# Attention loads in half as many DMAs, score tiles ahead of the maxima, first loads in another order

## The reference

```python
x = _layernorm(x + _L0_attn_ref(x, ...))       # causal self-attention
x = _layernorm(x + _L0_xattn_ref(x, ctx_768, ...))   # attention to the context
x = _layernorm(x + _L0_ffn_ref(x, ...))        # soft mixture: 8 experts x 128 slots
x = _layernorm(x + _L1_attn_ref(x, ...))       # causal
x = _layernorm(x + _L1_xattn_ref(x, ctx_768, ...))   # context
x = _layernorm(x + _L1_ffn_ref(x, ...))        # x + causal attention, then + top-2 of 8 experts
```

## Time and profile before

| | |
|---|---|
| median of 3 runs | 3067.17 us (3059.79 to 3073.33) |
| the profiled execution | 3064.33 us, its span 3062.5 us |
| PE busy | 2568.9 us, 84% |
| DVE busy | 1499.4 us, 49% |
| ACT busy | 1346.1 us, 44% |
| POOL busy | 457.8 us, 15% |
| mean granted clock of PE, share of full speed | 0.916 |
| DMA, mean over the span | 85 GB/s |

### The profile page before, as it was taken

How to read it: one execution, slowest core, us unless ns; L and a number is a source line. 1 busy time by engine, 2 the same in 40 slices (tenths; PEclk the granted TensorE clock), 3 DMA queues, 4 the chain that set the end, 5 groups by cost and what they waited for, 6 DMA issues and landing times. The chain is left out here.

```text
span 3062.5 us, 48054 instructions
## 1 busy us (share of the span) xinstructions
PE 2568.9 (84%) x15793; PEld 1469.9 (48%) x15794; DVE 1499.4 (49%) x4196; ACT 1346.1 (44%) x2886; POOL 457.8 (15%) x719
## 2 busy tenths in 40 slices
PE   4999999999828979998588999898987986489992
PEld 2555544444314446676355544343434554356671
DVE  0555677888425420013444487777744564222223
ACT  2555456666634432211244456665754553022220
POOL 3222212101110000000112212212122000500004
PEclk7899999999969999999699999999998997599996
DMA  8344664454000012203644465354422332711102
GB/s 205 97 126 126 131 118 82 68 73 73 1 17 1 1 59 88 87 17 137 158 109 123 111 128 80 56 101 62 92 59 60 103 83 95 249 31 34 34 30 89
DMA packets 184550, 259.98 MB, mean 85 GB/s; under 512 B 32952, under 2 KB 106944, under 8 KB 184256
## 3 DMA queue, kind: packets, MB, share of 16 engines
q1 hardware_dynamic: 181264, 248.85, 34.5%
q0 software_dynamic: 3072, 8.39, 0.9%
HBM read 180.71 MB, written 81.53 MB: 86 GB/s over the span
## 5 line engine op out<-in xcount | busy, mean ns | idle before, releaser
L1345 ACT ACTIVATE second_p<-psum 128x512 f32<-128x512 f32 (+3 forms) x1024 | 461.7, 520 | 287.9 <-PE psum L1211 284.3
L1345 ACT ACTIVATE first_p<-psum 128x512 f32<-128x512 f32 (+3 forms) x768 | 365.7, 547 | 179.1 <-PE psum L1211 176.5
L1419 DVE TENSOR_REDUCE first_max_parts<-psum 128x1 f32<-128x512 f32 x512 | 323.0, 684 | 74.7 <-PE psum L1188 72.1
L1419 DVE TENSOR_REDUCE second_max_parts<-psum 128x1 f32<-128x512 f32 x512 | 321.9, 683 | 72.9 <-PE psum L1188 70.2
L1415 DVE CUSTOM_DVE_ANT_0 second_masked<-psum,mask_qk 128x384 f32<-128x384 f32 (+3 forms) x512 | 230.0, 489 | 230.7 <-PE psum L1188 189.1
L1201 PE MATMUL psum<-second_q,second_k 64*128 64x512 f32 (+3 forms) x1024 | 227.7, 440 | 42.1 <-DVE second_max_parts L1419 26.2
L1188 PE MATMUL psum<-second_k,second_q 64*128 64x512 f32 (+3 forms) x1024 | 203.7, 395 | 67.5 <-DMA second_k<-a_k_parts 51.5
L1223 PE MATMUL psum<-second_p,second_v_aug 128*32 128x512 f32 (+3 forms) x2048 | 240.1, 542 | 8.3 <-ACT second_p L1345 8.1
L1188 PE MATMUL psum<-first_k,first_q 64*128 64x512 f32 (+3 forms) x768 | 158.0, 411 | 61.7 <-ACT first_held L1382 26.0
L1201 PEld LDWEIGHTS psum<-second_q,second_k 64*128 64x128 f32 x1024 | 98.8, 188 | 230.1 <-issue 83.6
L1415 DVE CUSTOM_DVE_ANT_0 first_masked<-psum,mask_qk 128x128 f32<-128x128 f32 (+3 forms) x256 | 114.8, 488 | 179.7 <-PE psum L1188 152.5
(11 more groups left out here) (317 smaller groups left out, 3819.2 us busy)
## 6 DMA issues: line engine op xcount, KB each, us to landing
first_k<-c_k_parts SPq DMA_DIRECT2D x128, 128.0 KB, 5.7
second_q<-a_q_parts SPq DMA_DIRECT2D x256, 64.0 KB, 2.8
second_k<-a_k_parts SPq DMA_DIRECT2D x256, 64.0 KB, 2.9
second_k<-c_k_parts SPq DMA_DIRECT2D x128, 128.0 KB, 5.6
first_q<-a_q_parts SPq DMA_DIRECT2D x128, 64.0 KB, 2.9
first_k<-a_k_parts SPq DMA_DIRECT2D x128, 64.0 KB, 2.9
c_k_parts<-first_held SPq DMA_DIRECT2D x16, 512.0 KB, 3.2
first_q<-c_q_parts SPq DMA_DIRECT2D x128, 64.0 KB, 5.3
```

Of the source, the lines that this page charges most:

```text
L1345: evacuated(act.activation(probs[tile % 2][:, 2 * h + p, q0:SEQ], bank[:, q0:SEQ], ACT.Exp, scale=scale), event)
L1419: evacuated(v.reduce_max(max_parts[n % 2][:, h, p, qt, k0 // BANK:k0 // BANK + 1], bank[:, 0:width], axis=AX_X), event)
```

## The change

Four edits.

1. The plan: a step writes both score tiles, then all its units, then the values of tile t-1 (or the last values and the drain of group n-1), and then the chain steps and pieces.
2. `load(n)` issues 8 DMAs in place of 16, each for 32 partitions. The weights' columns (and biases) of queries and keys are put in another order on the host (`by_heads`), so that the two heads of a row pair follow each other within a partition; the buffer holds the two contiguously (`keys_of`). A group's bytes stay the same, and so do the matmuls.
3. The weights: in the first stage the first layer's are issued at the start as before, the others at a new event "weights", which stands after load 2; in the second all stand after loads 0 to 3. In the first stage load 0 and vload 0 now stand after the first slot's projections, the other first loads after the second slot's. The first contexts are loaded later.
4. `stage_experts`: two semaphores in place of one, so that the first matmul waits for the up matrix and its bias alone.

```diff
         for t in range(steps):
             plan.append(("scores", n, (t, 0)))
-            share(units, 2 * t + 1, 2 * steps)
-            if t:
-                plan.append(("values", n, t - 1))
-            elif n:
-                plan.extend([("values", n - 1, layer_of(n - 1).key_tiles - 1), ("drain", n - 1, 0)])
             if t == 1:
                 if n:
                     plan.append(("turn", n - 1, 0))
...
             plan.append(("scores", n, (t, 1)))
             share(units, 2 * t + 2, 2 * steps)
+            if t:
+                plan.append(("values", n, t - 1))
+            elif n:
+                plan.extend([("values", n - 1, layer_of(n - 1).key_tiles - 1), ("drain", n - 1, 0)])
...
+        def keys_of(n):
+            keys = layer_of(n).keys
+            return ks[n % NB][:, :, :].rearrange("p i t -> p (i t)")[:, 0:2 * keys].rearrange("p (i t) -> p i t", i=2)
...
-                for dst, src, columns in own_loads:
-                    sp.dma_start(dst, src, allow_slow_non_contiguous=columns).then_inc(own_in, 16)
-                for dst, src, columns in later_loads:
-                    sp.dma_start(dst, src, allow_slow_non_contiguous=columns).then_inc(later_in, 16)
+                def fetch_weights(loads, done):
+                    for dst, src, columns in loads:
+                        sp.dma_start(dst, src, allow_slow_non_contiguous=columns).then_inc(done, 16)
+
+                if not layers[0].projected:
+                    fetch_weights(own_loads, own_in)
...
-                        for blk, (qp, kp) in enumerate(((0, 0), (0, 1), (1, 0), (1, 1))):
-                            at = slice(64 * h + HD * blk, 64 * h + HD * (blk + 1))
-                            sp.dma_start(qs[n % NB][at, :, :].bitcast(F32),
-                                         q_dram[qp, row:row + 2 * HD, :].rearrange("(i d) t -> d i t", d=HD)
-                                         ).then_inc(stack_in[n % NB], 16)
-                            sp.dma_start(ks[n % NB][at, :, 0:layer.keys].bitcast(F32),
-                                         k_dram[kp, row:row + 2 * HD, :].rearrange("(i d) t -> d i t", d=HD)
-                                         ).then_inc(stack_in[n % NB], 16)
+                        for half in range(2):
+                            at = slice(64 * h + 2 * HD * half, 64 * h + 2 * HD * (half + 1))
+                            sp.dma_start(qs[n % NB][at, :, :].bitcast(F32).rearrange("p i t -> p (i t)"),
+                                         q_dram[half, row:row + 2 * HD, :].rearrange("(d i) t -> d (i t)", i=2)
+                                         .unsqueeze(0).to_broadcast([2, HD, 2 * SEQ])
+                                         ).then_inc(stack_in[n % NB], 16)
+                            sp.dma_start(ks[n % NB][at, :, :].rearrange("p i t -> p (i t)")[:, 0:2 * layer.keys].bitcast(F32),
+                                         k_dram[:, row:row + 2 * HD, :].rearrange("a (d i) t -> a d (i t)", i=2)
+                                         ).then_inc(stack_in[n % NB], 16)
...
+                    elif event[0] == "weights":
+                        if layers[0].projected:
+                            fetch_weights(own_loads, own_in)
+                        fetch_weights(later_loads, later_in)
...
-                        pe.wait_ge(stack_in[r], 256 * (n // NB + 1))
+                        pe.wait_ge(stack_in[r], 128 * (n // NB + 1))
...
-        pieces = {-3: front_pieces(a0, 0, "x") + FIRST_LOADS, -2: front_pieces(a0, 1, "x")}
+        pieces = {-3: front_pieces(a0, 0, "x") + FIRST_LOADS[:2],
+                  -2: front_pieces(a0, 1, "x") + FIRST_LOADS[2:5] + [("weights", 0, 0), ("load", 3, 0)]}
...
-        contexts = {-3: [("context", BATCH, 0), ("context", BATCH + 1, 0)]}
+        contexts = {-1: [("context", BATCH, 0), ("context", BATCH + 1, 0)]}
...
-        pieces = {-3: FIRST_LOADS}
-        contexts = {-3: [("context", BATCH, 0), ("context", BATCH + 1, 0)]}
+        pieces = {-3: FIRST_LOADS + [("weights", 0, 0)]}
+        contexts = {-2: [("context", BATCH, 0), ("context", BATCH + 1, 0)]}
```

More of the change, by code:

```diff
@@ L1188, in unit @@
                         ins = pe.matmul(bank_of(event, h)[:, 0:width], qs[r][own, p, qt * P:(qt + 1) * P],
-                                        ks[r][own, p, k0:k0 + width], start=True, stop=True)
+                                        keys_of(n)[own, p, k0:k0 + width], start=True, stop=True)
                         filled(ins, event)
@@ L1200, in scores @@
                         own = slice(64 * h, 64 * h + 64)
-                        pe.matmul(bank_of(event, h)[:, q0:SEQ], ks[r][own, p, t * P:(t + 1) * P],
+                        pe.matmul(bank_of(event, h)[:, q0:SEQ], keys_of(n)[own, p, t * P:(t + 1) * P],
                                   qs[r][own, p, q0:SEQ], start=True, stop=False)
@@ L1563, in stage_experts @@
         hidden = sb("hidden", [P, HM, BANK])
-        w_in = [c.sem(f"{name}_w_in{i}") for i in range(2)]
+        up_in, down_in = [c.sem(f"{name}_up_in{i}") for i in range(2)], [c.sem(f"{name}_down_in{i}") for i in range(2)]
         s_up, s_gelu = c.sem(f"{name}_up"), c.sem(f"{name}_gelu")
         s_down, s_read = c.sem(f"{name}_down"), c.sem(f"{name}_read")
-        per_load = 16 * 4
+        per_load = 16 * 2
         tiles = BANK // P
@@ L1584, in body @@
                     one = bass.ds(e, 1)
-                    sp.dma_start(up[r][:, :, :], w1[one, :, :].rearrange("o (k p) n -> p (o k) n", p=P)).then_inc(w_in[r], 16)
-                    sp.dma_start(up_bias[r][:, :], b1[one, :, :].rearrange("o p m -> p (o m)")).then_inc(w_in[r], 16)
-                    sp.dma_start(down[r][:, :, :], w2[one, :, :].rearrange("o (m p) n -> p (o m) n", p=P)).then_inc(w_in[r], 16)
+                    sp.dma_start(up[r][:, :, :], w1[one, :, :].rearrange("o (k p) n -> p (o k) n", p=P)).then_inc(up_in[r], 16)
+                    sp.dma_start(up_bias[r][:, :], b1[one, :, :].rearrange("o p m -> p (o m)")).then_inc(up_in[r], 16)
+                    sp.dma_start(down[r][:, :, :], w2[one, :, :].rearrange("o (m p) n -> p (o m) n", p=P)).then_inc(down_in[r], 16)
                     wait_for(sp, s_read, tiles * (e - 1))
                     sp.dma_start(down_bias[r][:, :], b2[one, :].rearrange("o n -> (o n)").partition_broadcast(P)
-                                 ).then_inc(w_in[r], 16)
+                                 ).then_inc(down_in[r], 16)
                 for_experts(sp, body)
@@ L1596, in body @@
                 def body(e, pair, r):
-                    pe.wait_ge(w_in[r], (pair + 1) * per_load)
+                    pe.wait_ge(up_in[r], (pair + 1) * per_load)
                     for m in range(HM):
@@ L1603, in body @@
                         ins.then_inc(s_up, 1)
+                    pe.wait_ge(down_in[r], (pair + 1) * per_load)
                     for t in range(tiles):
@@ L1617, in body @@
                 def body(e, pair, r):
[L1618 removed]
+                    act.wait_ge(up_in[r], (pair + 1) * per_load)
                     wait_for(act, s_down, e * tiles)
@@ L1629, in body @@
                 def body(e, pair, r):
-                    v.wait_ge(w_in[r], (pair + 1) * per_load)
+                    v.wait_ge(down_in[r], (pair + 1) * per_load)
                     for t in range(tiles):
@@ L2289, in by_groups, with by_heads @@
     return np.concatenate([others, own], axis=-1)
+HEADED = {"L0_attn_w_attn": 2, "L0_attn_b_attn": 2, "L1_attn_w_qkv": 2}
+HEADED.update({f"{layer}_{x}": 1 for layer, names in (("L0_xattn", ("Wq", "Wk", "bq", "bk")), ("L1_xattn", ("wq", "wk", "bq", "bk")),
+                                                      ("L1_ffn", ("Wq", "Wk", "bq", "bk"))) for x in names})
+def by_heads(a, blocks):
+    own, rest = a[..., :blocks * D], a[..., blocks * D:]
+    own = own.reshape(own.shape[:-1] + (-1, 2, HD)).swapaxes(-2, -1).reshape(own.shape)
+    return np.concatenate([own, rest], axis=-1)
 def kernel(**inputs):
@@ L2303 @@
             a = by_groups(a, name in TURNED_ROWS)
+        if name in HEADED:
+            a = by_heads(a, HEADED[name])
         if name == "ctx_768":
```

## The result

The kernel after takes 3861.35 us (median of 4 runs, 3856.75 to 3862.2) against 3069.82 for the kernel before beside it: a ratio of 1.258, 95% interval 1.255 to 1.262. The forecast of 3690 (3450 to 3900) named the side and the cause; it is 171 us short.

The account below looks back on a forecast made before the run. The prediction took TensorE, busy 2568.9 of 3062.5 us, as the bound, with late loads counting in full. 3064.3 + 577 (stretches) + 18 + 44 (starts) - 14 (tails) - 3 (experts) = 3686, forecast 3690 us, range 3450 to 3900.

Parts of the forecast that it names:

- The two engines: Query and key loads: an outermost dimension of 2 lets each DMA reach only 2 of 16 engines.
- The rate and the chain: Group loads: two engines give 48.9 GB/s, each load waits for the one before; periods 25.9 us causal, 38.1 cross.
- The stretches: Five runs of causal or cross groups between drains, each group lengthened to the load period: together +577 us.
- groups that were longer than the new period for their pieces' sake would add some more (left out): In the five stretches: groups already longer than the load period add some time, given no size.
- The third rival: Slot changes: split stores queue behind loads on the two engines, one cross load each at four changes, +129: 3815 us; chance 0.10.
- The starts: Before each stage's first drain: first loads run one after another on two engines, +18 us first stage, +44 second.
- a value bias among those weights: Second stage's start: the first values need the value bias among weights landing about 1543; first drain near 1554, not 1510.
- The tails: Last two groups of each stage, no units or loads left: the new order saves 14 us in all.
- The first rival: Group loads: they still use 16 engines, so the early loads pay, about 2958 us; chance 0.17.
- the order: Steps of the attention groups: scores first, then units, values later; bounded by -40 and +40 us alone.
- the fewer issues: DMA waits within the loops, if loads use 16 engines: about 37 of 45.9 us go.
- Its threshold of three engines: Group loads: from three engines upward, periods of 18.7 and 27.4 us are about what groups take now.

Follow-up runs that it names:

- e1: The kernel after, its same 8 loads a group turned so that the 16 rows of a head stand outermost: 2979.97 us, ratio 0.972.
- e2: The kernel before with the change's 8 loads a group and nothing else of the change: 3934.25 us, ratio 1.284.
- e11: The kernel after, each load cut into two DMAs with 8 rows outermost, 16 DMAs a group: 3136.07 us, ratio 1.023.
- e10: The kernel after with load n+3 at the head of group n, so two loads can be under way: 3509.19 us, ratio 1.145.
- e3: The kernel after with no piece written in step 0 of a group, each piece one step later: 3752.67 us, ratio 1.224.
- e9: The kernel of e1 with the old order of a step in every group that still has units to place: 2940.21 us, ratio 0.960.
- e5: The kernel before with the 8 merged loads of e1 (16 rows outermost) and nothing else of the change: 2991.01 us, ratio 0.975.
- e6: The kernel before with the reordered weights, first loads and contexts alone, 16 loads a group: 3036.11 us, ratio 0.990.
- e7: The kernel after with query loads as 16-row DMAs, keys still on an outermost 2, 12 DMAs a group: 3356.65 us, ratio 1.094.

## Why the prediction was right, and where its sizes were off

**The two engines: right, shown.** The completions count it (19200), e1 undoes it, e2 does it alone. By the rule of the Trainium skill (page "DMA: Bandwidth & Descriptors", section "Why a DMA increments its semaphore by 16 and not by 1") 2 engines were to be expected, and 8 in e11; both counts agree (13752 and 22712 small packets).

**The rate and the chain: right, and so close in part by luck.** Two engines gave 51.0 GB/s (e10) against 48.9, so 1 MB takes 20.55 us for 21.5; the fixed part of the chain is 2.8 + 2.4 us against 4.4. The two errors cancel: 25.77 for 25.9, and cross groups without pieces 37.5 to 38.4 for 38.1. That no two loads overlap held too (e10 let them, and won 352 us).

**The stretches: +741 in place of +577.** The term that was sized wrongly is "groups that were longer than the new period for their pieces' sake would add some more (left out)". The excess is 164 us, in the order of the sum 55, 11, 37, 19 and 42. By the drains of before, the groups longer than the new period exceed it by only 48 us in all. Most of the rest comes from groups that were shorter: any piece in step 0 stands between the unit and the next load's issue (9.0 us in the group shown, not 2.8). e3 moves those pieces and takes 106 of the 164 back. The 58 that it leaves (9, -2, 18, 2 and 31 by stretch) are near the 48 of the longer groups (0, 0, 14, 4 and 30); the other 10 are open. The third rival looked for an excess in the stores; e3 makes the same stores, so they are not the larger part.

**The starts: +25 and +37 for +18 and +41**, the latter with the experts' -3 in it (their first matmul waits 8.3 us, 12.4 before). SP's own issues were not in the sum. At the second start many issues of a 128 KB load last some 2.3 us once a group's loads are under way, and the weights stand behind 32 of them. The prediction had the first values wait for a value bias among those weights. Layer a1 has none: its one weight is the output matrix `a_wo`, and `augment`, which does not use it, waits for it through the layer's common semaphore. From the timeline of after:

```profile
1785.80 0.66 SPq L1035 DMA_DIRECT2D second_q<-a_q_parts  x1
...
1851.86 2.31 SPq L1039 DMA_DIRECT2D second_k<-a_k_parts  x1
1854.21 2.28 SPq L1001 DMA_DIRECT2D second_a_wo<-in_L_attn_w_o  x1
...
1871.83 1.41 POOL L1106 TENSOR_TENSOR second_v_aug<-second_v_raw,second_a_bv 128x256 f32<-128x256 f32 x2 [81.07 <-DMA second_a_wo<-in_L_attn_w_o]
1872.70 1.94 PE L1234 MATMUL psum<-second_p,second_v_aug 128*32 128x512 f32 x8 [19.38 <-POOL second_v_aug L1106]
```

**The tails: -10 for -14.** The sum, 741 + 25 + 37 - 10 = 793, is what the spans differ by, 3855.0 - 3062.5 = 792.5.

**The first rival, had it held,** was put at 2958; e1, which makes its condition true, gives 2980. Three of its terms were off: the order was taken at -20 and costs some 40 in the loops (e9 against e1), the fewer issues were taken at 37 and bring 76 (e5), the starts at 49 without the experts and bring 31 (e6). Its threshold of three engines was taken from mean group lengths, by which periods of 18.7 and 27.4 us do no harm. e7 has periods near those (17.2 to 18.9 and 28.2 to 30.1) and loses 289 us.

## What to carry to other kernels

Read a DMA's outermost dimension on both sides before its bytes: here it was worth 881 us to put the dimension of 16 outermost and the broadcast or the pair second. Merging DMAs pays (76 us here) once that is kept. When a load becomes the bound, count everything that the written order places between the first reader of one load and the issue of the next, on every engine that walks the list. And hold a new period against the shortest groups, not the mean.

## What was not expected of the hardware

A DMA issue on SP took 0.42 us for 16 partitions of two 2 KB rows (before), 0.59 for 32 partitions of 4 KB on 16 engines (e1) or, while few loads were under way, on 2 (after), and 0.65 for the 16-partition loads of e11.

PE's granted clock fell where loads made it wait, and was still low when PE was busy again. Three windows of after (columns as above, the clock third from the end): in a wait, right behind it, and ahead of it.

```profile
182.71:193.13 10.42, 0.44 (x6) 0.13 (x5) 0.59 (x2) 1.91 (x4) 0.00 (x0) 0.66 0.24 96
193.13:199.41 6.28, 6.28 (x24) 2.92 (x25) 1.24 (x10) 1.85 (x3) 0.00 (x0) 0.50 0.06 19
177.00:182.00 5.00, 5.00 (x42) 2.78 (x44) 1.91 (x9) 2.42 (x7) 1.28 (x1) 1.00 0.37 145
```

At 0.50, the lower of the two levels (1.2 of 2.4 GHz), the projection at 194.33 takes 3.78 us; the next of the same line, at 202.12 and a granted clock of 1.00, takes 1.98. PE's busy time rose by 148 us for the same 15793 matmuls; this projection's share of it lies inside the chain.
